# Gated linear attention with 64 routed experts on one core: the expert steps on two shared projection banks and two expert banks, with the down projection one slot later

## The reference

```python
# attention branch: 8 heads, keys of 128, values of 64, gates with a decay
q = xn @ Wq; k = (xn @ Wk) * DK ** -0.5; v = xn @ Wv
alpha = sigmoid((xn @ Wg + bg) / 16)            # one decay per token and head
state = alpha_t * state + k_t v_t^T; out_t = q_t @ state      # over the tokens
attn = (out * sigmoid(xn @ Wog)) @ Wo
# expert branch: 64 experts, 8 per token out of 4 of 8 groups, 256 slots per expert
scores = sigmoid(xn @ gate_w.T)                 # top 8 of the allowed groups, weights scaled by 2.5
y = (silu(X @ w_gate) * (X @ w_up)) @ w_down    # X: the up to 256 tokens of the expert, in order
ffn = sum over a token's experts of weight * y
return x + attn + ffn
```

## Time and profile before

| | |
|---|---|
| time, median of 3 runs | 1458.67 us (1458.36 to 1460.96) |
| profiled execution | 1454.37 us, span 1452.7 us, mean granted TensorE clock 0.976 |
| TensorE busy | 1320.8 us, 91% of the span (weight loads 1143.8 us beside it) |
| VectorE busy | 960.7 us, 66% |
| ScalarE busy | 552.4 us, 38% |
| GpSimd busy | 530.6 us, 37% |
| transfers | 203.5 MB, mean 140 GB/s |

### The profile page before, as it was taken

How to read it: one execution, slowest core, us unless ns; L and a number is a source line. 1 busy time by engine, 2 the same in 40 slices (tenths; PEclk the granted TensorE clock), 3 DMA queues, 4 the chain that set the end, 5 groups by cost and what they waited for, 6 DMA issues and landing times.

```text
span 1452.7 us, 27616 instructions
## 1 busy us (share of the span) xinstructions
PE 1320.8 (91%) x9460; PEld 1143.8 (79%) x9460; DVE 960.7 (66%) x2425; ACT 552.4 (38%) x1079; POOL 530.6 (37%) x407
## 2 busy tenths in 40 slices
PE   2999888998989899989999999999999999999992
PEld 2778777786878687778888888888888888888872
DVE  4766777867775666857757577575775757757450
ACT  4555555545554342223333333333333333333220
POOL 3001001000100006735636456364563645636422
PEclk9989999999999999999999999999999999999996
DMA  5338433434332131125646566465564655646666
GB/s 201 128 124 266 137 122 125 163 106 135 124 136 96 66 94 59 59 84 152 150 138 154 130 152 148 135 154 133 148 147 136 156 135 154 151 140 151 178 216 219
DMA packets 134513, 203.48 MB, mean 140 GB/s; under 512 B 12400, under 2 KB 106160, under 8 KB 134320
## 3 DMA queue, kind: packets, MB, share of 16 engines
q1 hardware_dynamic: 108208, 161.10, 34.3%
q0 software_dynamic: 26240, 41.63, 14.9%
HBM read 153.33 MB, written 57.74 MB: 145 GB/s over the span
## 4 chain that ended last, share of the span: by engine, by line
PE 66%; DVE 15%; issue 6%; DMA 5%; ACT 4%; SPq 1%; POOL 1%; DVEq 1%; POOLq 0%; ACTq 0%
PE bank L672 16%; PE bank L791 6%; PE bank L747 6%; PE bank L767 6%; PE bank L684 5%; PE bank L714 4%; PE bank L732 4%; PE bank L800 4%; PE bank L696 3%; PE bank L735 3%; PE bank L705 3%; DMA out_dram<-arena 3%; DVE Dt L1251 2%; PE bank L617 2%; PE bank L781 2%
## 5 line engine op out<-in xcount | busy, mean ns | idle before, releaser
L540 POOL DMA_INDIRECT arena<-table,idx_all x132 | 167.7, 1270 | 271.6 <-DVE arena L1354 208.7
L548 POOL DMA_INDIRECT acc<-arena,idx_all x128 | 224.9, 1757 | 78.3 <-DMA acc<-arena,idx_all 42.2
L672 PE MATMUL bank<-xp,wq 128*128 128x512 f32 x768 | 210.2, 409 | 0.0
L672 PE MATMUL bank<-xp,wk 128*128 128x512 f32 x768 | 208.1, 407 | 0.0
L672 PEld LDWEIGHTS bank<-xp,wk 128*128 128x128 f32 x768 | 142.4, 192 | 32.0 <-issue 0.2
L1251 DVE TENSOR_TENSOR_SCAN Dt<-decay,eye_b 128x512 f32<-128x512 f32 x128 | 156.7, 1226 | 2.3 <-DMA decay<-decay_dram 2.3
L672 PEld LDWEIGHTS bank<-xp,wq 128*128 128x128 f32 x768 | 137.6, 191 | 25.5
L714 PE MATMUL bank<-qT,kT 128*128 128x128 f32 x1024 | 136.8, 277 | 2.7 <-ACT kT L954 2.7
L747 PEld LDWEIGHTS bank<-V,kw 128*128 128x128 f32 x960 | 121.0, 193 | 15.1 <-issue 10.6
L714 PEld LDWEIGHTS bank<-qT,kT 128*128 128x128 f32 x1024 | 125.2, 193 | 5.0 <-ACT kT L954 4.5
L747 PE MATMUL bank<-V,kw 128*128 128x64 f32 x960 | 128.2, 277 | 0.0
(11 more groups left out here) (152 smaller groups left out, 2200.0 us busy)
## 6 DMA issues: line engine op xcount, KB each, us to landing
decay<-decay_dram SPq DMA_DIRECT2D x64, 512.0 KB, 5.5
carry<-decay_dram SPq DMA_DIRECT2D x60, 512.0 KB, 4.6
arena<-in_L_attn_x_dram SPq DMA_DIRECT2D x16, 512.0 KB, 4.5
table<-arena SPq DMA_DIRECT2D x16, 512.0 KB, 3.0
xT_dram<-arena SPq DMA_DIRECT2D x16, 512.0 KB, 3.0
xs<-xT_dram SPq DMA_DIRECT2D x16, 512.0 KB, 5.3
arena<-in_L_ffn_w_gate_dram SPq DMA_DIRECT2D x64, 128.0 KB, 4.8
arena<-in_L_ffn_w_up_dram SPq DMA_DIRECT2D x64, 128.0 KB, 4.8
```

The costliest lines, as they stand in the source:

```text
L540: pool.indirect_dma_start(out=xg[:, e % 2, j, :], out_offset=None, in_=table[:, :], in_offset=bass.IndirectOffsetOnAxis(ap=idx_all[:, e, j ...
L548: pool.indirect_dma_start(out=acc[:, :], out_offset=bass.IndirectOffsetOnAxis(ap=idx_all[:, e, j:j + 1], axis=0), in_=yb[:, e % 2, j, :], ...
L672: last = mm(bank[which][:, :], w[:, part, k, h * DK:(h + 1) * DK], xp[:, other, k, :], start=(k + i == 0), stop=(k == KD - 1 and i == 2))
```

## The change

In expert steps (and the last) the projections no longer have banks of their own: in the order in which they are made (`turns`) they take `bank[0]` and `bank[1]` in turns, and each waits for the copy of the projection two turns before (`bank_free`). `bank[4]` becomes a second expert bank: experts take `bank[7]` and `bank[4]` in turns, and the transposes of an expert wait for `y_cp` of the expert two before. In a slot the hidden products come after both projections, and the down projection of an expert follows the next slot's scores, ahead of the next expert's transposes; the last expert of a step has it in the next step behind `scores(c, 0)`:

```diff
+        turns = [("v", 0), ("q", 0), ("v", 1), ("k", 0), ("v", 2), ("v", 3)]
+        for h in range(1, H + 1):
+            turns += [("q", h)] if h < H else []
+            turns += [("og", og_slots("experts").index(h))] if h in og_slots("experts") else []
+            turns += [("k", h)] if h < H else []
+
+        def bank_of(kind, what, i):
+            if kind in ("experts", "last"):
+                return bank[turns.index((what, i)) % 2]
+            return bank[{"q": 0, "k": 1, "v": 4, "og": 4}[what]]
+
+        def bank_free(eng, c, kind, what, i):
+            n = turns.index((what, i)) - 2
+            if n < 0:
+                eng.wait_ge((qk_cp, og_cp)[n + 2], (16 * c, 4 * c)[n + 2])
+                return
+            before, k = turns[n]
+            if before == "v":
+                eng.wait_ge(v_cp, 4 * c + k + 1)
+            elif before == "og":
+                eng.wait_ge(og_cp, 4 * c + k + 1)
+            else:
+                eng.wait_ge(qk_cp, at(c, 16, 2 * k + (before == "k") + 1))
+
+        expert_bank = (bank[7], bank[4])
...
-            def proj_qk(c, h, which):
+            def proj_qk(c, kind, h, which):
                 u = 2 * h + which
                 w = (wq, wk)[which]
-                if not (isinstance(c, int) and at(c, 16, u) < 2):
+                to = bank_of(kind, "qk"[which], h)
+                if kind in ("experts", "last"):
+                    bank_free(pe, c, kind, "qk"[which], h)
+                elif not (isinstance(c, int) and at(c, 16, u) < 2):
                     pe.wait_ge(qk_cp, at(c, 16, u) - 1)
                 for k in range(KD):
                     for i, (part, other) in enumerate(PARTS):
-                        last = mm(bank[which][:, :], w[:, part, k, h * DK:(h + 1) * DK], xp[:, other, k, :],
+                        last = mm(to[:, :], w[:, part, k, h * DK:(h + 1) * DK], xp[:, other, k, :],
...
-                else:
-                    pe.wait_ge(kw_cp, at(c, 8, 1))
+                if not isinstance(e, int) or e > 1:
+                    pe.wait_ge(y_cp, e - 1)
+                elif e == 1:
+                    pe.wait_ge(og_cp, 4 * c)
                 for k in range(KD):
                     for half in range(NHALF):
                         lo = k * CAP + half * P
-                        last = tr(bank[7][:, lo:lo + P], xg[:, j % 2, half, k * P:(k + 1) * P], ident[:, :])
+                        last = tr(expert_bank[j % 2][:, lo:lo + P], xg[:, j % 2, half, k * P:(k + 1) * P], ident[:, :])
...
-                if kind == "experts" and s > 0 and place != 2:
-                    {0: expert_tokens, 1: expert_hidden, 3: expert_down}[place](c, s - 1)
+                if kind == "experts" and s > 0 and place == 0:
+                    if s > 1:
+                        expert_down(c, s - 2)
+                    expert_tokens(c, s - 1)
+                if kind == "experts" and s > 0 and place == 2:
+                    expert_hidden(c, s - 1)
...
-                proj_v(c, 3)
+                if kind in ("experts", "last") and not (isinstance(c, int) and c == E0):
+                    expert_down(c - 1, STEP_E - 1)
+                proj_v(c, kind, 3)
                 if not first:
...
-                        proj_og(c, og_slots(kind).index(s))
-                    if s < H and kind == "experts" and s % 2 == 0:
-                        proj_qk(c, s, 1)
+                        proj_og(c, kind, og_slots(kind).index(s))
                     beside(c, kind, s, 1)
-                    if s < H and not (kind == "experts" and s % 2 == 0):
-                        proj_qk(c, s, 1)
+                    if s < H:
+                        proj_qk(c, kind, s, 1)
                     beside(c, kind, s, 2)
...
-            with pe.Fori(E0, E1) as c:
+            step(E0, "experts")
+            with pe.Fori(E0 + 1, E1) as c:
...
-                if kind == "experts" and s > 0 and place < 2:
-                    (expert_tokens, expert_gate)[place](c, s - 1)
-                if kind == "experts" and place == 1 and 0 < s < H:
-                    weights_high_e(c, s)
+                if kind == "experts" and s > 0 and place == 0:
+                    expert_tokens(c, s - 1)
+                if kind == "experts" and s > 0 and place == 2:
+                    expert_gate(c, s - 1)
+                    if s < H:
+                        weights_high_e(c, s)
...
                     if s == H and kind != "last":
                         tokens_high(c + 1)
-                    if s < H and kind == "experts" and s % 2 == 0:
-                        qk_copy(c, s, 1)
                     beside(c, kind, s, 1)
-                    if s < H and not (kind == "experts" and s % 2 == 0):
-                        qk_copy(c, s, 1)
+                    if s < H:
+                        qk_copy(c, kind, s, 1)
...
-                if kind == "experts" and s == 0 and place == 3:
-                    weights_low_e(c, 0)
                 if kind == "experts" and s > 0:
                     if place == 0:
-                        tokens_low_e(c, s - 1)
+                        if s > 1:
+                            expert_out(c, s - 2)
+                            tokens_low_e(c, s - 1)
                     if place == 2:
                         expert_hidden(c, s - 1)
                         if s < H:
                             weights_low_e(c, s)
-                    if place == 3:
-                        expert_out(c, s - 1)
...
+                    if s == 1 and kind in ("experts", "last") and not (isinstance(c, int) and c == E0):
+                        expert_out(c - 1, STEP_E - 1)
+                    if s == 1 and kind == "experts":
+                        weights_low_e(c, 0)
                     if s == 1 and not is_first(c) and not is_last(c):
                         projected(c, 2, kind)
+                        if kind == "experts":
+                            tokens_low_e(c, 0)
                         projected(c, 3, kind)
                     if s % 2 and not is_first(c):
                         ends_kept(c, s // 2)
-                    if s == 1 and kind in ("experts", "count"):
+                    if s == 1 and kind == "count":
                         beside(c, kind, 0, 3)
```

More of the change, by code:

```diff
@@ L683, in proj_v, with proj_og @@
                     for i, (part, other) in enumerate(PARTS):
-                        last = mm(bank[4][:, :], xp[:, part, k, b * P:(b + 1) * P], wv[:, other, k, :],
+                        last = mm(to[:, :], xp[:, part, k, b * P:(b + 1) * P], wv[:, other, k, :],
                                   start=(k + i == 0), stop=(k == KD - 1 and i == 2))
                 last.then_inc(v_ps, 1)
-            def proj_og(c, j):
-                if j > 0:
+            def proj_og(c, kind, j):
+                to = bank_of(kind, "og", j)
+                if kind in ("experts", "last"):
+                    bank_free(pe, c, kind, "og", j)
+                elif j > 0:
                     pe.wait_ge(og_cp, 4 * c + j)
@@ L695, in proj_og @@
                     for i, (part, other) in enumerate(PARTS):
-                        last = mm(bank[4][:, :], wog[:, part, k, j * P:(j + 1) * P], xp[:, other, k, :],
+                        last = mm(to[:, :], wog[:, part, k, j * P:(j + 1) * P], xp[:, other, k, :],
                                   start=(k + i == 0), stop=(k == KD - 1 and i == 2))
@@ L790, in expert_hidden @@
                         for i, (part, other) in enumerate(PARTS):
-                            last = mm(bank[7][:, m * CAP:(m + 1) * CAP], wgu_p[:, part, m, k * I:(k + 1) * I],
+                            last = mm(expert_bank[j % 2][:, m * CAP:(m + 1) * CAP], wgu_p[:, part, m, k * I:(k + 1) * I],
                                       xgT[:, other, k * CAP:(k + 1) * CAP], start=(k + i == 0),
@@ L799, in expert_down @@
                 for half in range(NHALF):
-                    last = mm(bank[7][:, half * D:(half + 1) * D], hT[:, half * P:(half + 1) * P],
+                    last = mm(expert_bank[j % 2][:, half * D:(half + 1) * D], hT[:, half * P:(half + 1) * P],
                               wde[:, j % 2, :], start=True, stop=True)
@@ L849, in step @@
                     if s < H:
[L850 removed]
+                        proj_qk(c, kind, s, 0)
                     if s == 1 and not first:
@@ L947, in select_group, with qk_copy @@
                    .then_inc(selc_ready, 1)
-            def qk_copy(c, h, which):
+            def qk_copy(c, kind, h, which):
                 act.wait_ge(qk_ps, at(c, 16, 2 * h + which + 1))
@@ L953, in qk_copy, with v_copy, og_gate @@
                 dst, scale = ((qT, 1.0), (kT, float(DK) ** -0.5))[which]
-                f(dst[:, h % 2, :], bank[which][:, :], ACT.Copy, scale=scale).then_inc(qk_cp, 1)
-            def v_copy(c, b):
+                f(dst[:, h % 2, :], bank_of(kind, "qk"[which], h)[:, :], ACT.Copy, scale=scale).then_inc(qk_cp, 1)
+            def v_copy(c, kind, b):
```

(18 more changed lines are left out.)

45 lines of the change are left out of this document (23 added, 22 removed).

## The result

The changed kernel takes **1450.34 us** (median; 1444.33 to 1454.63, 11 runs) against 1458.67 (1453.51 to 1469.91, 11 runs, alternating on one chip). The ratio is 0.9927 (95% interval 0.9907 to 0.9946), or -10.6 us. The forecast was 1447.7. On a second chip the same code measured 1452.50 (12 runs) against 1458.98 (17 runs): ratio 0.9962 (0.9946 to 0.9978), -5.5 us. The two intervals touch only at their ends: the gain is clear of the noise on both chips, its size is not the same. (The ratio is not that of the two medians; these are 8.3 us apart on the first chip and 6.5 on the second.)

What follows compares the result with a forecast made beforehand. TensorE's own instruction stream was taken to bound the expert steps. Removed waits -27, new waits +11 and the end +5 sum to -11 us, from a median of 1458.7 to 1447.7; own range 1442 to 1454 (55%), 8 in 10 1437 to 1460.

Steps and rivals of the forecast that it cites:

- The waits that go: TensorE in expert steps: waits of hidden products, transposes and keys removed, all 27 us; projections on two banks cost nothing.
- The step without waits: Expert step added up from TensorE's pieces: 87.4 us against 90.7 measured, so 3.35 us a step to gain.
- The new wait: Hidden products wait for low tokens in slots 8 and 4: 1.35 us a step, 11 us in all (2 to 30).
- my T + 6.7 to 8.85: Landing time of the next expert's weights, T being the next slot's start; in slot 3 up to T + 10.35.
- my upper bound of 2.3: Slot 8's new wait at most, with weights at T + 8.85; taken as 1.05 us a step with restart.
- nothing on top: GpSimd's gather and scatter released 3 to 4 us later in the slot: no cost beyond slot 8's wait.
- signs that I had named for a wrong forecast: Steps over 90 us with waits in slots 4 and 7; projections waiting for copies; transposes waiting for gathers; end starting early.
- the sign of being right: Among the signs: hidden products still wait for low tokens, once a step, in slot 8; steps of 88.7 us.
- slot 4's term: Hidden products in slot 4 wait for low tokens: 0.3 us with the restart, bounds 0 and 1.0.
- The end: Copies after TensorE: first summed store 6.7 us later, next round at most half of 6.63 saved; +5 us (+3.3 to +6.7).
- The weight loads pull ScalarE and VectorE: Rival: late loads make slots 4, 7 and 8 lose 3.8 us a step; +10 us, 1469; chance 12%.
- Nothing comes back: Rival: waits go, loads land at 3.2, slot 8 costs 0.3 to 0.6 a step; -20 us, 1439; chance 22%.

Runs made afterwards that it cites:

- Experiment 1: Changed kernel with the last expert's down projection and scaled output back at the end of slot 8: 1451.94 us, ratio 0.9963 to before.
- Experiment 2: Changed kernel with VectorE's scaled queries of slots 3 and 7 made one slot later, behind the low tokens: 1441.72 us, ratio 0.9897 to before.
- experiment 3: Changed kernel with weight loads waiting for the split weights instead of the down projection, `w_down` in four buffers: 1468.48 us, ratio 1.0075 to before.
- experiments 1, 2, 3 and 6: The 6 here: changed kernel with the edits of Experiment 1 and Experiment 2 together, 1439.60 us, ratio 0.9869 to before.

## Why the prediction came out right

**The waits that go: right.** Those of the hidden products in slots 1 and 7, of the transposes for the expert output and of the keys are gone from the list, and no projection (L701, L731) waits for a copy, so two banks are enough.

**The step without waits: 87.4 predicted, about 86.9.** Less their waits and restarts, six of the eight steps come to 86.8 to 86.9 us (the first with its moved down projection counted in), the last to 87.2, and the sixth to 88.4, by the 1.5 us at the lower clock. The slot with no wait and the pieces of the earlier trace rows differ in one: down behind scores costs 0.86 us instead of the 0.92 behind an update, eight times a step. This gain of 0.5 us I had not seen.

**The new wait: right in place and mechanism, mis-sized.** Predicted 1.35 us a step (slot 8 1.05, slot 4 0.3), measured (15.9 + 15 x 0.24) / 8 = 2.4: slot 8 1.85, slot 4 0.6. The term that was mis-sized is the start of slot 8's chain. I let VectorE begin the low weights 8.28 us after slot 7's start, when its own products are done, with the load landed by then. The trace has the load issued at 976.15, and ScalarE, which waits for it, starts at 980.63, 4.5 us later. In six steps ScalarE starts 7.9 to 8.3 us into slot 7, in the second 8.6 and in the sixth 8.9; VectorE follows 0.67 later, at 8.5 to 9.6. All but the sixth load came within my T + 6.7 to 8.85, but I had taken the low half of it. The two late ones make slot 8 wait 2.12 and 2.32 us, with the restart past my upper bound of 2.3, and the longer wait is the one that ended at the lower clock, a cost that the prediction had at nothing. From the load on the chain was exact. Slot 4's waits are 0.18 to 0.77, and one of eight has none; with the restart that reaches the upper bound of 1.0.

**GpSimd: "nothing on top" held in one profile of two.** In the first profile of after TensorE's matmuls wait for no gather, in the second for 4.6 us in nine places, 6.8 with the restarts. There two of the signs that I had named for a wrong forecast are met: steps of over 90 us (90.3 on average) with waits in slots 4 and 7 too, and transposes that wait for a gather. In both profiles the hidden products (L826) wait in slot 4 as well, where the sign of being right was one wait a step.

The median landing of the loads of `w_gate` is 4.8 us on the page of before and 2.6 on that of after, but the two are not of the same loads: in the expert steps the profile of before shows the landings of loads issued in odd slots and at a step's start, that of after those of even slots. For the third load after has 2.2 to 3.7 us in even slots; in slot 7 it is 4.1 to 4.7, and 5.4 in the sixth step, counted to ScalarE's start. The Trainium skill's fit (DMA: Bandwidth & Descriptors, "Anatomy of one DMA — SWDGE (gpsimd) path"), an estimate of 2.3 us, is for transfers by way of GpSimd, and these loads are SyncE's. It is near the fastest of the even slots (slot 2: 2.2 to 2.7) and far from slot 7, which decides. By the page slot 4's term would have gone; it was 0.6.

**The end: right in mechanism, 4.0 against 5.** The first summed store is gated by the sum. It leaves 6.2 us after it otherwise could (at 1383.08; the carry load passed its wait at 1375.82, and 1.1 us later the store could have followed), predicted 6.7. Its transfer takes 3.9 us where it took 6.63, as its companion store is long done: 2.7 saved, predicted "at most half". Experiment 1 shows the place; the medians leave the size open.

**The sum.** With the measured terms a step changes by -3.35 - 0.5 + 2.4 = -1.45 us, eight by -11.6. The profiles differ by -9.3, 0.3 us a step less; 0.2 of this is the place at the lower clock and the longer last step, the rest is not accounted for. The end's +4.0 and +1.3 in the opening (the same code, so no effect of the change) leave -4.0 between the two profiles, and -5.3 without the opening. The forecast of -11 lies at the first chip's -10.6 and is double the second's -5.5. That the number fell so close is partly luck: three of its terms were off, not all to one side (-0.5 us a step for the down projection, +1.1 for the new wait, the end 1 us less), the account by stages of the two profiles gives only half of it, and with the second chip's gain the time would have been 1453.

**The rivals.** "The weight loads pull ScalarE and VectorE" is half there: ScalarE's wait is 15.6 us in total (I had expected more than the 21.4 of the earlier trace rows: wrong), but part of it sits in slot 7, where it counts in full. "Nothing comes back" did not happen: 2.4 us a step came back. Experiment 2 comes near that rival's 1439 only by moving one instruction more: 1441.7.

## What to carry to other kernels

Before moving an expert's stage past a wait, add up the chain of the engine that feeds it (here VectorE, 5.08 us from the weights) and look for a link that nobody needs yet: moving the scaled queries one slot gave 4 to 9 us (0.9897 against 0.9927 and 0.9962), nearly as much as the whole reordering. An order and the banks that it needs are one change: alone they gave +12 and -5 us. A transfer whose wait ends earlier is not one that starts earlier or costs less: look at what stands ahead of it in its queue and which others it now meets. And look past a mean clock of 1.00: one wait of 2.3 us was followed by a group at half the clock.

## What the runs showed of the hardware that was not expected

In the output slots 2, 4 and 6 of the expert steps, what waits for the last output matmul goes on 0.05 us (VectorE) and 0.18 us (SyncE) after its end in all four profiles of kernels whose down projection stands at the end of its own slot (before twice, banks only, order only) and in the first of after. In the second profile of after and in experiments 1, 2, 3 and 6 VectorE is 1.0 to 1.5 us behind in these slots and SyncE 0.13 more, from the first expert step on, in all but 5 of 120 places. The same code did both, in two executions on two chips; it was seen with the down projection one slot later only (5 of 6 profiles, against 0 of 4). The expert output of slots 3, 5 and 7, and with it the gather for the expert after the next, then come 1.1 to 1.3 us later, and slot 8's transposes wait about 0.5 us for it. It fits the steps of 90.3 us instead of 89.4 and the weaker ratio of the second chip; no run took the late event out by itself. The ends of matmuls in the trace are modelled, so the late event may be the matmul or its signal. What brings it about was not found and stays open.

After a wait of TensorE of 2.32 us in after and of 2.03, 2.37 and 2.17 us in experiment 3 the granted clock was 0.50 over the next group (in after) or the one behind it (in experiment 3, where the transposes came first); after a wait of 2.12 us in after it stayed at 1.00. The means by stretch, 1.00 and 0.99, do not show it.
